# A dense feed-forward in three float32r passes over split weights, inside a two-layer attention and expert kernel

## The chip, the cores and the metric

The kernel runs as one launch on 1 core of a Trainium2 chip. The metric is the time of the launch on the device in microseconds (us), the median of several runs.

## What is computed

The reference takes x (4 x 512 tokens of 512) through four residual steps: a map attention, a token-choice block, a cross attention over 16 heads, and a routed feed-forward with 32 experts. Each takes a layer norm of x. The change lies in the token-choice block, whose dense feed-forward is the last part of this cut:

```python
k = max(1, int(T * CAPACITY))                       # 64 of 512 tokens of each of 4 batches
_, idx = jax.lax.top_k(scores, k)
...
x = sel.reshape(S, D)                               # S = 256 picked rows, D = 512
...                                                 # attention of 16 query and 8 key heads
x1 = x + attn_out
h2 = _rms_norm(x1, ln2_w)
mlp = jax.nn.silu(h2 @ w_gate) * (h2 @ w_up) @ w_down     # 512 x 2048, 512 x 2048, 2048 x 512
processed = x1 + mlp
gated = gate * processed + (1.0 - gate) * x
output = hidden_states.at[b, idx].set(gated.reshape(B, k, D))
```

All inputs and outputs are float32.

## The kernel before

The program is a row of stages (`build`), each with one block of instructions for every engine: `load_constants`, `map_attention`, `token_choice_ffn`, `project_heads`, `context_attention`, `routed_ffn`. X stays in SBUF from stage to stage. At the end of a block all engines meet, and the next block's instructions start together. Inside a block each engine works through its own list in order, and semaphores with increasing counts tie the lists to each other. PSUM is used as 8 banks of 128 x 512 float32.

`token_choice_ffn` (L344) has three blocks. The first picks the 256 rows. The second is the attention, one key head at a time (8 heads); SP loads the slices of `w_o` for it into two buffers (L577) and waits for `out_ready` before it refills one. The third is the dense part (from L736), 256 rows as two groups of 128:

- SP issues all 12 weight loads at once, 1 MB each: for each of 4 parts (512 of the 2048 inner columns) a quarter of `w_gate` and `w_up` (L756) and of `w_down` (L757). All three tensors lie whole in SBUF.
- `rms_turned` (from L504) writes h2 transposed into `b_hT`: ScalarE squares the rows (L513), VectorE and GpSimd make the scale (L521, L529), VectorE scales (L524), TensorE turns 8 blocks (L535), ScalarE multiplies by the norm's weights on the way out of PSUM (L516).
- TensorE, for part n: the gate product into banks 0 and 1, the turn of part n - 1's middle (L819) into banks 4 and 5, the up product into banks 2 and 3 (both L811), and part n - 1's down product (L827) into banks 6 and 7, which add up over all parts. A product is 8 matmuls: 2 groups by 4 slices of 128 of the contraction, each a stationary 128 x 128 block of `b_hT` (or `b_midT`) and 512 moving columns of weights. They are float32; the trace holds two MATMUL records for each.
- ScalarE, in a loop over the parts: silu of the gate product into `b_act_g` (L797), then the turned middle from PSUM into `b_midT` (L801). VectorE, in a loop: `b_mid` = `b_act_g` times the up product (L771).
- Behind the last down product VectorE adds and gates (L776 to L781), TensorE spreads the rows back over the tokens (L848), and VectorE adds them to X (L785).

The routed stage of the same kernel works in float32r already: a number is split into a high part (its float32r rounding, written by a cast) and a low part (the rest, by a subtraction), and a product is three matmuls, high by high, high by low and low by high (L2230, L2235, L2250, L2255).

## Time and profile before

| | us |
|---|---|
| median of 3 runs | 2389.5 (2388.86 to 2392.63) |
| the profiled execution | 2395.94 |
| its span, first to last instruction | 2394.2 |
| TensorE busy | 1989.2 |
| VectorE busy | 1155.8 |
| ScalarE busy | 543.5 |
| mean granted TensorE clock | 0.909 |

The profile is of one execution. PE is TensorE, PEld its weight loads, DVE VectorE, ACT ScalarE, POOL GpSimd, SP SyncE; a q behind a name is the engine's queue of issued instructions. In rows of the trace, `out<-in` names what an instruction writes and reads, and an idle time in brackets is followed by what ended it. Matmuls are pipelined, so the duration of one is longer than the distance to the next; the pace is read from starts. The granted clock is a share of 2.4 GHz. `b_x` in a row stands for `b_x1`.

### The profile page before, as it was taken

How to read it: one execution, taken by the hardware profiler on the slowest of the kernel's cores; microseconds unless marked ns; L12 is line 12 of the kernel's file. 1: busy time of each engine (PE TensorE's matmuls, PEld its weight loads, DVE VectorE, ACT ScalarE, POOL GpSimd, SP SyncE). 2: the span in 40 equal slices, each digit the busy share in tenths (PEclk: the TensorE clock that was granted, in tenths of full speed). 3: DMA queues.
4: the chain of work that ended last, by engine and by line, in shares of the span. 5: the costliest groups of instructions: out<-in, count | busy, mean ns of one | idle time of the engine just before them, and what ended most of it. 6: DMA issues, size and time to landing. Idle time of an engine off the chain costs nothing.

```text
span 2394.2 us, 33404 instructions
## 1 busy us (share of the span) xinstructions
PE 1989.2 (83%) x10468; PEld 1422.6 (59%) x10469; DVE 1155.8 (48%) x2197; ACT 543.5 (23%) x1151; POOL 1141.4 (48%) x566
## 2 busy tenths in 40 slices
PE   5946887969854889999589999999999999999910
PEld 3424443424322333333379999999999999999810
DVE  2564442057673566774773444444444554443300
ACT  3221221101112444443112221122222122222100
POOL 0000000003562455563435557667666878781886
PEclk8977997979985789999789999999999999999965
DMA  3051004121125346711124435554555545543999
GB/s 111 0 147 61 18 27 162 58 80 49 63 83 174 117 163 226 237 51 41 40 88 162 182 118 167 174 159 152 161 163 163 176 160 188 177 163 90 207 158 196
DMA packets 199485, 305.96 MB, mean 128 GB/s; under 512 B 16472, under 2 KB 94808, under 8 KB 199416
## 3 DMA queue, kind: packets, MB, share of 16 engines
q1 hardware_dynamic: 141624, 187.24, 24.8%
q0 software_dynamic: 21504, 50.93, 9.4%
q10 hardware_dynamic: 36288, 66.84, 7.9%
q8 instruction: 45, 0.74, 0.1%
q14 instruction: 24, 0.20, 0.0%
HBM read 186.42 MB, written 118.55 MB: 127 GB/s over the span
## 4 chain that ended last, share of the span: by engine, by line
PE 41%; POOL 5%; DVE 2%; DMA 1%; issue 1%; POOLq 0%; ACT 0%; DVEq 0%
PE psum L2230 16%; PE psum L2250 8%; PE psum L2235 8%; POOL X L1954 5%; PE psum L2255 4%; PE psum L2217 3%; PE psum L2224 2%; DMA X<-d_y,f_slots 1%; DVE f_arena L1175 1%; DVE e_gu_low L2144 0%; DVE f_arena L1165 0%; DVE f_arena L1174 0%; DVE f_arena L1183 0%; DVE e_gu_low L2079 0%; POOLq L1791 0%
## 5 line engine op out<-in xcount | busy, mean ns | idle before, releaser
L2230 PE MATMUL psum<-e_gu_high,e_rowT_high 128*128 (+1 forms) x1272 | 428.0, 339 | 6.3 <-DVE e_gu_low L2144 3.8
L2230 PE MATMUL psum<-e_gu_low,e_rowT_high 128*128 (+1 forms) x1272 | 408.6, 323 | 0.0
L2235 PE MATMUL psum<-e_gu_high,e_rowT_low 128*128 (+1 forms) x1272 | 256.1, 323 | 22.0 <-DVE e_rowT_low L2034 22.0
L1973 ACT ACTIVATE e_silu<-psum 128x352 f32<-128x352 f32 x159 | 73.7, 464 | 879.4 <-PE psum L2235 873.9
L2230 PEld LDWEIGHTS psum<-e_gu_high,e_rowT_high 128*128 128x128 f32 x1272 | 240.7, 189 | 31.1 <-issue 27.0
L2230 PEld LDWEIGHTS psum<-e_gu_low,e_rowT_high 128*128 128x128 f32 x1272 | 241.6, 190 | 3.8
L2235 PEld LDWEIGHTS psum<-e_gu_high,e_rowT_low 128*128 128x128 f32 x1272 | 213.7, 189 | 22.3 <-DVE e_rowT_low L2034 22.3
L2045 DVE TENSOR_TENSOR e_midT_low<-psum,e_midT_high 128x256 fp32r<-128x256 f32 x159 | 67.5, 424 | 325.6 <-ACT e_midT_high L1982 323.4
L2250 PE MATMUL psum<-e_d_high,e_midT_high 128*128 (+3 forms) x477 | 187.7, 394 | 1.0 <-ACT e_midT_high L1982 1.0
L2250 PE MATMUL psum<-e_d_low,e_midT_high 128*128 (+3 forms) x477 | 188.4, 395 | 0.0
L1954 POOL DMA_INDIRECT X<-d_y,f_slots x96 | 148.1, 1542 | 83.3 <-DVE f_arena L2065 52.8
L1904 POOL TENSOR_TENSOR e_gu_high<-f_gu_in,e_ones 128x1408 fp32r<-128x1408 f32 x32 | 81.1, 2534 | 196.2 <-PE psum L2235 178.6
L2065 DVE COPY f_arena<-psum 128x512 f32<-128x512 f32 x127 | 87.8, 692 | 143.4 <-PE psum L2255 140.1
L1405 DVE TENSOR_REDUCE f_hs<-psum 128x2 f32<-128x992 f32 x128 | 151.3, 1182 | 0.0
L1936 POOL DMA_INDIRECT d_sorted<-f_hs,f_slots x96 | 93.7, 976 | 101.8 <-DMA d_sorted<-f_hs,f_slots 63.4
L942 POOL TENSOR_TENSOR x_hrstd<-x_hrstd,minus_half 128x64 f32<-128x64 f32 x8 | 92.3, 11535 | 96.3 <-DVE x_hrstd L960 96.3
L2255 PE MATMUL psum<-e_d_high,e_midT_low 128*128 (+3 forms) x477 | 137.8, 397 | 0.1
L529 POOL TENSOR_TENSOR b_r_ms<-b_r_ms,minus_half 128x2 f32<-128x2 f32 x2 | 1.4, 695 | 241.7 <-DVE b_r_ms L521 241.7
L2034 DVE TENSOR_TENSOR e_rowT_low<-psum,e_rowT_high 128x512 fp32r<-128x512 f32 x159 | 107.7, 677 | 0.0
L2040 DVE SCALAR_TENSOR_TENSOR e_picked<-e_row,f_arena 128x6 f32<-128x6 f32 x127 | 104.2, 821 | 0.0
L1908 POOL TENSOR_TENSOR e_gu_low<-f_gu_in,e_gu_high 128x1408 fp32r<-128x1408 f32 x32 | 103.2, 3225 | 0.0
L1911 POOL TENSOR_TENSOR e_gu_low<-f_gu_in,e_gu_high 128x1408 fp32r<-128x1408 f32 x32 | 102.9, 3216 | 0.0
(348 smaller groups left out, 3787.6 us busy)
## 6 DMA issues: line engine op xcount, KB each, us to landing
d_sorted<-f_hs SPq DMA_DIRECT2D x32, 1048.0 KB, 9.6
e_row<-d_sorted ACTq DMA_DIRECT2D x125, 262.0 KB
d_y<-f_arena ACTq DMA_DIRECT2D x127, 256.0 KB
f_gu_in<-in_L_ffn_w_gate SPq DMA_DIRECT2D x32, 704.0 KB, 5.2
f_gu_in<-in_L_ffn_w_up SPq DMA_DIRECT2D x32, 704.0 KB, 5.1
f_d_in<-in_L_ffn_w_down SPq DMA_DIRECT2D x32, 512.0 KB
d_y<-f_hs SPq DMA_DIRECT2D x8, 1024.0 KB, 5.7
f_d_in<-in_L_ffn_w_down SPq DMA_DIRECT2D x32, 192.0 KB
```

The costliest lines, as they stand in the source:

```text
L942: nc.gpsimd.tensor_tensor(hrstd[:, a, :], hrstd[:, a, :], c.minus_half[:, 0:JT * H], ALU.pow).then_inc(hrstd_ready, 1)
L1405: nc.vector.reduce_max(to[:, :, 0], banks[:, :, 0:MAIN], AX.X, negate=True).then_inc(max_ready, 1)
L1908: nc.gpsimd.tensor_tensor(gu_low[:, par, :, 0:M], gu_in[:, :, 0:M], gu_high[:, par, :, 0:M].bitcast(F32), ALU.subtract).then_inc(gate_spli ...
L1911: nc.gpsimd.tensor_tensor(gu_low[:, par, :, M:2 * M], gu_in[:, :, M:2 * M], gu_high[:, par, :, M:2 * M].bitcast(F32), ALU.subtract).then_i ...
L1936: nc.gpsimd.indirect_dma_start(c.dram["d_sorted"], bass.IndirectOffsetOnAxis(ap=slots[:, k, t:t + 1], axis=0), hs[:, t, :], None).then_inc ...
L1954: nc.gpsimd.indirect_dma_start(c.X[:, t, :], None, c.dram["d_y"], bass.IndirectOffsetOnAxis(ap=slots[:, k, t:t + 1], axis=0), compute_op=A ...
L2034: nc.vector.tensor_tensor(rowT_low[par][:], XT.rearrange("p (k n) -> p k n", k=CC), rowT_high[par][:].bitcast(F32), ALU.subtract).then_inc ...
L2040: nc.vector.scalar_tensor_tensor(picked[par][:], row[par][:, D + TOPK:ROW], expert, row[par][:, D:D + TOPK], ALU.is_equal, ALU.mult, accum ...
L2230: nc.tensor.matmul(bank[:, 0:M].unsqueeze(1), rowT_high[par][:, k, :], w[:, bass.ds(buffer, 1), k, at:at + M], start=(k == 0 and n == 0), ...
L2235: last = nc.tensor.matmul(bank[:, 0:M].unsqueeze(1), rowT_low[par][:, k, :], gu_high[:, bass.ds(buffer, 1), k, at:at + M], start=False, st ...
L2250: nc.tensor.matmul(Y[par].unsqueeze(1), midT_high[0:n, k, :], w[0:n, bass.ds(buffer, 1), k, :], start=(k == 0 and m == 0), stop=False)
L2255: last = nc.tensor.matmul(Y[par].unsqueeze(1), midT_low[0:n, k, :], d_high[0:n, bass.ds(buffer, 1), k, :], start=False, stop=(k == ME - 1))
```

## The change

The 12 slices of the weights become 12 pieces of one size in the order in which TensorE uses them (`PIECES`). A piece is loaded into one of 4 raw buffers; ScalarE casts it to float32r in one of 4 high buffers, VectorE writes raw minus high into one of 4 low buffers, and TensorE makes each product from 24 float32r matmuls: 16 with the high part of `b_hT` (or of the middle) against high and low weights in turn, then 8 with its low part against the high weights. `b_hT` and the middle are split likewise: a cast by ScalarE, a subtraction by VectorE. The lists of ScalarE and VectorE are now written out, without a loop. The first two raw buffers are held from the stage's start, and SP issues their loads in the attention block, behind the third slice of `w_o`. In the dense part SP waits, from piece 4 on, until the low of the piece four before is written. A cast waits for its load, and from piece 4 on for the product of the piece four before.

```diff
@@ -364,6 +368,21 @@
         heads_held = kept.enter_context(ExitStack())
         w_heads = sbuf(nc, heads_held, "b_w_heads", [P, CC, KVH, HEAD_COLS])
         heads_loaded, = sems(nc, c, "b_", "heads_loaded")
+        PARTS = INNER // 512
+        PIECES = [("gate", 0), ("up", 0)]
+        for n in range(1, PARTS):
+            PIECES += [("gate", n), ("up", n), ("down", n - 1)]
+        PIECES += [("down", PARTS - 1)]
+        RAW, RING, EARLY = 4, 4, 2
+        raw = [far_sbuf(nc, kept, f"b_raw{n}", [P, 4, 512]) for n in range(EARLY)]
+        raw_loaded = sems(nc, c, "b_", " ".join(f"raw{n}_loaded" for n in range(RAW)))
+
+        def load_piece(sp, p):
+            kind, n = PIECES[p]
+            cols = slice(n * 512, (n + 1) * 512)
+            src = c.dram["L0_ffn_w_" + kind]
+            src = src[cols, :] if kind == "down" else src[:, cols]
+            sp.dma_start(raw[p % RAW][:], src.rearrange("(k p) n -> p k n", p=P)).then_inc(raw_loaded[p % RAW], 16)
 
         with ExitStack() as stack:
             hs = sbuf(nc, stack, "b_hs", [P, NT, D])
@@ -537,7 +556,7 @@
                 last.then_inc(turned, 1)
                 pe.wait_ge(hT_ready, 1)
 
-            return on_act, on_dve, on_pool, on_pe
+            return on_act, on_dve, on_pool, on_pe, hT_ready
 
         with ExitStack() as stack:
             w_o = sbuf(nc, stack, "b_w_o", [P, 2, QH, D])
...
@@ -576,6 +595,9 @@
                         sp.wait_ge(out_ready, h - 1)
                     sp.dma_start(w_o[:, h % 2], c.dram["L0_ffn_wo"][h * QH * DH:(h + 1) * QH * DH, :].rearrange(
                         "(q d) n -> d q n", d=DH)).then_inc(wo_loaded[h % 2], 16)
+                    if h == 2:
+                        for p in range(EARLY):
+                            load_piece(sp, p)
 
             @block.gpsimd
             def _(pool):
@@ -734,28 +756,27 @@
         heads_held.close()
 
         with ExitStack() as stack:
-            PARTS = INNER // 512
-            w_gate = sbuf(nc, stack, "b_w_gate", [P, CC, INNER])
-            w_up = sbuf(nc, stack, "b_w_up", [P, CC, INNER])
-            w_down = sbuf(nc, stack, "b_w_down", [P, INNER // P, D])
+            raw += [sbuf(nc, stack, f"b_raw{n}", [P, 4, 512]) for n in range(EARLY, RAW)]
+            high, low = [[sbuf(nc, stack, f"b_w_{part}{n}", [P, 4, 512], F32R) for n in range(RING)] for part in ("high", "low")]
             act_g = sbuf(nc, stack, "b_act_g", [P, GROUPS, 512])
             mid = sbuf(nc, stack, "b_mid", [P, GROUPS, 512])
-            midT = sbuf(nc, stack, "b_midT", [P, GROUPS, 512])
-            part_loaded = sems(nc, c, "b_", " ".join(f"part{n}_loaded" for n in range(PARTS)))
+            midT_high, midT_low = [sbuf(nc, stack, f"b_midT_{part}", [P, GROUPS, 512], F32R) for part in ("high", "low")]
+            hT_high, hT_low = [sbuf(nc, stack, f"b_hT_{part}", [P, CC, SLOTS], F32R) for part in ("high", "low")]
             gated, upped, silu_ready, mid_ready, mid_turned, midT_ready, out_ready = sems(
                 nc, c, "b_", "gated upped silu_ready mid_ready mid_turned midT_ready mlp_ready")
             chain_dve, diff_ready, spread, landed = sems(nc, c, "b_", "chain3 diff_ready spread landed")
+            piece_high, piece_low, hT_high_ready, hT_low_ready, midT_low_ready = sems(
+                nc, c, "b_", "piece_high piece_low hT_high_ready hT_low_ready midT_low_ready")
             block = stack.enter_context(nc.Block())
-            rms_act, rms_dve, rms_pool, rms_pe = rms_turned(stack, "b_r2_", x1, mid, 1)
+            rms_act, rms_dve, rms_pool, rms_pe, hT_written = rms_turned(stack, "b_r2_", x1, mid, 1)
 
             @block.sync
             def _(sp):
-                for n in range(PARTS):
-                    cols = slice(n * 512, (n + 1) * 512)
-                    for dst, src in ((w_gate, c.dram["L0_ffn_w_gate"]), (w_up, c.dram["L0_ffn_w_up"])):
-                        sp.dma_start(dst[:, :, cols], src.rearrange("(k p) n -> p k n", p=P)[:, :, cols]).then_inc(part_loaded[n], 16)
-                    sp.dma_start(w_down[:, n * 4:(n + 1) * 4, :], c.dram["L0_ffn_w_down"].rearrange("(k p) n -> p k n", p=P)[
-                        :, n * 4:(n + 1) * 4, :]).then_inc(part_loaded[n], 16)
+                for p in range(EARLY, len(PIECES)):
+                    if p >= RAW:
+
+                        sp.wait_ge(piece_low, p - RAW + 1)
+                    load_piece(sp, p)
 
             @block.gpsimd
             def _(pool):
@@ -763,15 +784,45 @@
 
             @block.vector
             def _(dve):
-                rms_dve(dve)
-                with dve.Fori(0, PARTS) as n:
+                def low_of(*pieces):
+                    for p in pieces:
+                        dve.wait_ge(piece_high, p + 1)
+                        nc.vector.tensor_tensor(low[p % RING][:], raw[p % RAW][:], high[p % RING][:].bitcast(F32), ALU.subtract).then_inc(piece_low, 1)
+
+                def multiply(n):
                     dve.wait_ge(silu_ready, n + 1)
                     dve.wait_ge(upped, n + 1)
                     for g in range(GROUPS):
                         last = nc.vector.tensor_tensor(mid[:, g, :], act_g[:, g, :], c.bank[2 + g][:], ALU.mult)
                     last.then_inc(mid_ready, 1)
+
+                def low_midT(n):
+                    dve.wait_ge(midT_ready, n + 1)
+                    for g in range(GROUPS):
+                        last = nc.vector.tensor_tensor(midT_low[:, g, :], c.bank[4 + g][:], midT_high[:, g, :].bitcast(F32), ALU.subtract)
+                    last.then_inc(midT_low_ready, 1)
+
+                low_of(0, 1)
+                rms_dve(dve)
+                dve.wait_ge(hT_high_ready, 1)
+                nc.vector.tensor_tensor(hT_low[:], hT[:], hT_high[:].bitcast(F32), ALU.subtract).then_inc(hT_low_ready, 1)
+                low_of(2, 3)
+                multiply(0)
+                low_of(4)
+                low_midT(0)
+                low_of(5)
+                multiply(1)
+                low_of(6, 7)
+                low_midT(1)
+                low_of(8)
+                multiply(2)
+                low_of(9, 10)
+                low_midT(2)
+                low_of(11)
+                multiply(3)
+                low_midT(3)
                 chain = Chain(dve, chain_dve)
-                dve.wait_ge(out_ready, 1)
+                dve.wait_ge(out_ready, PARTS)
                 for g in range(GROUPS):
                     last = nc.vector.tensor_tensor(x1[:, g, :], x1[:, g, :], c.bank[6 + g][:], ALU.add)
                 chain.link(last)
@@ -789,57 +840,102 @@
 
             @block.scalar
             def _(act):
-                rms_act(act)
-                with act.Fori(0, PARTS) as n:
+                def high_of(*pieces):
+                    for p in pieces:
+                        act.wait_ge(raw_loaded[p % RAW], 16 * (p // RAW + 1))
+                        if p >= RING:
+
+                            kind, n = PIECES[p - RING]
+                            act.wait_ge({"gate": gated, "up": upped, "down": out_ready}[kind], n + 1)
+                        nc.scalar.copy(high[p % RING][:], raw[p % RAW][:]).then_inc(piece_high, 1)
+
+                def silus(n):
                     act.wait_ge(gated, n + 1)
-
                     for g in range(GROUPS):
                         last = nc.scalar.activation(act_g[:, g, :], c.bank[g][:], ACT.Silu)
                     last.then_inc(silu_ready, 1)
+
+                def copy_midT(n):
                     act.wait_ge(mid_turned, n + 1)
                     for g in range(GROUPS):
-                        last = nc.scalar.copy(midT[:, g, :], c.bank[4 + g][:])
+                        last = nc.scalar.copy(midT_high[:, g, :], c.bank[4 + g][:])
                     last.then_inc(midT_ready, 1)
+
+                high_of(0, 1)
+                rms_act(act)
+                act.wait_ge(hT_written, 1)
+                nc.scalar.copy(hT_high[:], hT[:]).then_inc(hT_high_ready, 1)
+                high_of(2, 3)
+                silus(0)
+                high_of(4)
+                copy_midT(0)
+                silus(1)
+                high_of(5, 6, 7)
+                copy_midT(1)
+                silus(2)
+                high_of(8, 9, 10)
+                copy_midT(2)
+                silus(3)
+                high_of(11)
+                copy_midT(3)
 
             @block.tensor
             def _(pe):
                 rms_pe(pe)
-
-                def product(at, w, n):
+                pe.wait_ge(hT_high_ready, 1)
+
+                def product(at, p):
+                    pe.wait_ge(piece_low, p + 1)
                     for g in range(GROUPS):
+                        rows = slice(g * P, (g + 1) * P)
                         for k in range(CC):
-                            last = nc.tensor.matmul(c.bank[at + g][:], hT[:, k, g * P:(g + 1) * P],
-                                                    w[:, k, n * 512:(n + 1) * 512], start=(k == 0), stop=(k == CC - 1))
+                            for m, w in enumerate((high, low)):
+                                nc.tensor.matmul(c.bank[at + g][:], hT_high[:, k, rows], w[p % RING][:, k, :], start=(k == 0 and m == 0), stop=False)
+                    pe.wait_ge(hT_low_ready, 1)
+                    for g in range(GROUPS):
+                        rows = slice(g * P, (g + 1) * P)
+                        for k in range(CC):
+                            last = nc.tensor.matmul(c.bank[at + g][:], hT_low[:, k, rows], high[p % RING][:, k, :], start=False, stop=(k == CC - 1))
                     return last
 
                 def turn_mid(n):
                     pe.wait_ge(mid_ready, n + 1)
+                    if n >= 1:
+                        pe.wait_ge(midT_low_ready, n)
                     for g in range(GROUPS):
                         for k in range(4):
                             last = nc.tensor.transpose(c.bank[4 + g][:, k * P:(k + 1) * P], mid[:, g, k * P:(k + 1) * P], c.ident[:])
                     last.then_inc(mid_turned, 1)
 
-                def down(n):
+                def down(n, p):
 
                     pe.wait_ge(midT_ready, n + 1)
+                    pe.wait_ge(piece_low, p + 1)
                     for g in range(GROUPS):
                         for k in range(4):
-                            last = nc.tensor.matmul(c.bank[6 + g][:], midT[:, g, k * P:(k + 1) * P], w_down[:, n * 4 + k, :],
-                                                    start=(n == 0 and k == 0), stop=(n == PARTS - 1 and k == 3))
+                            for m, w in enumerate((high, low)):
+                                nc.tensor.matmul(c.bank[6 + g][:], midT_high[:, g, k * P:(k + 1) * P], w[p % RING][:, k, :],
+                                                 start=(n == 0 and k == 0 and m == 0), stop=False)
+                    pe.wait_ge(midT_low_ready, n + 1)
+                    for g in range(GROUPS):
+                        for k in range(4):
+                            last = nc.tensor.matmul(c.bank[6 + g][:], midT_low[:, g, k * P:(k + 1) * P], high[p % RING][:, k, :],
+                                                    start=False, stop=(n == PARTS - 1 and k == 3))
                     return last
 
...
+                for p, (kind, n) in enumerate(PIECES):
+                    if kind == "gate":
+                        if n >= 1:
+                            pe.wait_ge(silu_ready, n)
+                        product(0, p).then_inc(gated, 1)
+                    elif kind == "up":
+                        if n >= 1:
+                            turn_mid(n - 1)
+                        product(2, p).then_inc(upped, 1)
+                    else:
+                        if n == PARTS - 1:
+                            turn_mid(n)
+                        down(n, p).then_inc(out_ready, 1)
```

Three places in the engines' lists, in the program's order (names as in the code, `x` the count, L the line of the kernel that is listed).

ScalarE in the dense part, before (L793 is the loop over the parts, so L797 and L801 run four times):

```order
L790 UNCONDITIONAL_BRANCH
L513 ACTIVATE b_mid,b_r_ms<-b_x 128x512 x2
L516 ACTIVATE b_hT<-psum,b_ln_w 128x256 x4
L793 UNCONDITIONAL_BRANCH
L793 ISA
L797 ACT_TABLE_LOAD
L797 ACTIVATE b_act_g<-psum 128x512 x2
L801 COPY b_midT<-psum 128x512 x2
```

and after (the start and the first two parts):

```order
L841 UNCONDITIONAL_BRANCH
L850 CAST b_w_high<-b_raw 128x2048 x2
L532 ACTIVATE b_mid,b_r_ms<-b_x 128x512 x2
L535 ACTIVATE b_hT<-psum,b_ln_w 128x256 x4
L867 CAST b_hT_high<-b_hT 128x1024
L850 CAST b_w_high<-b_raw 128x2048 x2
L855 ACT_TABLE_LOAD
L855 ACTIVATE b_act_g<-psum 128x512 x2
L850 CAST b_w_high<-b_raw 128x2048
L861 CAST b_midT_high<-psum 128x512 x2
L855 ACTIVATE b_act_g<-psum 128x512 x2
L850 CAST b_w_high<-b_raw 128x2048 x3
```

Two casts of weights stand ahead of the squares, one of `b_hT` behind its writing, and the others between silu and the copy of the middle.

VectorE at the same place, before:

```order
L764 UNCONDITIONAL_BRANCH
L521 TENSOR_SCALAR b_r_ms<-b_r_ms 128x2
L524 TENSOR_SCALAR b_mid<-b_x,b_r_ms 128x512 x2
L767 UNCONDITIONAL_BRANCH
L767 ISA
L771 TENSOR_TENSOR b_mid<-b_act_g,psum 128x512 x2
```

and after:

```order
L785 UNCONDITIONAL_BRANCH
L790 TENSOR_TENSOR b_w_low<-b_raw,b_w_high 128x2048 x2
L540 TENSOR_SCALAR b_r_ms<-b_r_ms 128x2
L543 TENSOR_SCALAR b_mid<-b_x,b_r_ms 128x512 x2
L808 TENSOR_TENSOR b_hT_low<-b_hT,b_hT_high 128x1024
L790 TENSOR_TENSOR b_w_low<-b_raw,b_w_high 128x2048 x2
L796 TENSOR_TENSOR b_mid<-b_act_g,psum 128x512 x2
L790 TENSOR_TENSOR b_w_low<-b_raw,b_w_high 128x2048
L802 TENSOR_TENSOR b_midT_low<-psum,b_midT_high 128x512 x2
```

Two subtractions stand ahead of the scale of the norm, and every later one between the two steps of the middle.

SP from the attention block to the dense part, after (before, the 8 loads of `w_o` stand together and the 12 weight loads behind them):

```order
L596 DMA b_w_o<-in_L_ffn_wo 128x2x512 x3
L385 DMA b_raw<-in_L_ffn_w_gate 128x4x512
L385 DMA b_raw<-in_L_ffn_w_up 128x4x512
L596 DMA b_w_o<-in_L_ffn_wo 128x2x512 x5
L561 UNCONDITIONAL_BRANCH
L773 UNCONDITIONAL_BRANCH
L385 DMA b_raw<-in_L_ffn_w_gate 128x4x512
L385 DMA b_raw<-in_L_ffn_w_up 128x4x512
L385 DMA b_raw<-in_L_ffn_w_down 128x4x512
```

The first two pieces come between `w_o`'s third and fourth slice, and the rest begin with piece 2.

## Rows read from the trace of the kernel before

**Rows 1.** The page, part 1: busy us (share of the span) x instructions.
```profile
PE 1989.2 (83%) x10468; PEld 1422.6 (59%) x10469; DVE 1155.8 (48%) x2197; ACT 543.5 (23%) x1151; POOL 1141.4 (48%) x566
```

**Rows 2.** Windows of the core: us, busy of each engine, granted clock, DMA share, GB/s.
```profile
393.50:404.30 10.80, 1.97 (x8) 1.57 (x8) 1.05 (x3) 4.18 (x9) 0.69 (x1) 0.53 0.90 323
404.30:498.00 93.70, 88.92 (x225) 40.88 (x226) 8.53 (x13) 12.49 (x19) 0.00 (x0) 0.97 0.26 97
404.30:426.00 21.70, 21.64 (x47) 9.56 (x48) 1.28 (x2) 1.08 (x2) 0.00 (x0) 0.92 1.05 387
1600.00:2000.00 400.00, 399.97 (x2365) 368.94 (x2364) 195.46 (x416) 81.04 (x236) 293.58 (x132) 1.00 0.52 166
```

**Rows 3.** Waits between 380 and 520 us: who <- whom: us, times, longest.
```profile
DVE b_mid L771 <- PE psum L811: 76.9, 4, 23.2
```

**Rows 4.** Timeline, 393 to 414 us: start, us, engine, line, operation, [idle before <-releaser].
```profile
393.75 0.63 ACT L513 ACTIVATE b_mid<-b_x 128x512 f32<-128x512 f32 x1 [7.73 <-PEq L542]
...
395.11 0.17 DVE L521 TENSOR_SCALAR b_r_ms<-b_r_ms 128x2 f32<-128x2 f32 x1 [1.67 <-ACT b_mid L513]
...
397.03 1.97 PE L535 MATMUL psum<-ident,b_mid 128*128 128x128 f32 x8 [4.91 <-DVE b_mid L524]
399.04 1.57 ACT L516 ACTIVATE b_hT<-psum,b_ln_w 128x256 f32<-128x256 f32 x4 [3.96 <-PE psum L535]
...
404.36 8.86 PE L811 MATMUL psum<-b_w_gate,b_hT 128*128 128x512 f32 x16 [5.36 <-DMA b_w_down<-in_L_ffn_w_down]
...
413.06 1.45 PE L811 MATMUL psum<-b_w_up,b_hT 128*128 128x512 f32 x3
```

**Rows 5.** Timeline of TensorE, 419 to 500 us.
```profile
419.92 7.03 PE L811 MATMUL psum<-b_w_gate,b_hT 128*128 128x512 f32 x16
426.79 1.04 PE L819 MATMUL psum<-ident,b_mid 128*128 128x128 f32 x8
427.66 7.03 PE L811 MATMUL psum<-b_w_up,b_hT 128*128 128x512 f32 x16
...
486.55 7.13 PE L827 MATMUL psum<-b_w_down,b_midT 128*128 128x512 f32 x16 [1.16 <-ACT b_midT L801]
```

**Rows 6.** Timeline of TensorE in the routed stage, the float32r down product.
```profile
1220.55 0.39 PE L2250 MATMUL psum<-e_d_high,e_midT_high 128*128 128x512 f32 x1
...
1221.94 0.87 PE L2255 MATMUL psum<-e_d_high,e_midT_low 128*128 128x512 f32 x3
```

**Rows 7.** Groups of ScalarE and VectorE by form: x count | busy us, mean ns | idle before.
```profile
L1977 ACT CAST e_rowT_high<-psum 128x512 fp32r<-128x512 f32 x159 | 96.2, 605 | 0.7 <-PE psum L2217 0.7
...
L2006 ACT CAST e_gu_high<-f_gu_in 128x1408 fp32r<-128x1408 f32 x2 | 2.7, 1388 | 0.0
...
L2006 ACT CAST e_d_high<-f_d_in 128x1024 fp32r<-128x1024 f32 x1 | 1.1, 1061 | 0.0
...
L2034 DVE TENSOR_TENSOR e_rowT_low<-psum,e_rowT_high 128x512 fp32r<-128x512 f32 x159 | 107.7, 677 | 0.0
...
L969 DVE TENSOR_TENSOR x_q<-x_q,x_affine 128x2048 f32<-128x2048 f32 x8 | 18.3, 2292 | 0.3
...
L2079 DVE TENSOR_TENSOR e_gu_low<-f_gu_in,e_gu_high 128x1408 fp32r<-128x1408 f32 x2 | 3.2, 1618 | 0.0
L2144 DVE TENSOR_TENSOR e_gu_low<-f_gu_in,e_gu_high 128x1408 fp32r<-128x1408 f32 x1 | 2.9, 2889 | 8.8 <-ACT e_gu_high L2009 8.8
...
L2079 DVE TENSOR_TENSOR e_d_low<-f_d_in,e_d_high 128x1024 fp32r<-128x1024 f32 x1 | 1.2, 1219 | 0.0
```

**Rows 8.** The tile b_w_gate: from issue to landing.
```profile
DMA to landing us min/median/max: 5.1/13.0/15.4
```

**Rows 9.** Line 687 (the w_o products): what its idle time waited for: us, times.
```profile
  ACT b_oT L662: 2.9, 2
```

**Rows 10.** Timeline of TensorE in the routed stage at the low clock.
```profile
1210.98 0.49 PE L2230 MATMUL psum<-e_gu_high,e_rowT_high 128*128 128x352 f32 x1
1211.27 0.49 PE L2230 MATMUL psum<-e_gu_low,e_rowT_high 128*128 128x352 f32 x1
```

More of the change, by code:

```diff
@@ L562, in token_choice_ffn @@
             block = stack.enter_context(nc.Block())
[L563 removed]
+            rms_act, rms_dve, rms_pool, rms_pe, _ = rms_turned(stack, "b_r1_", picked, qkv[:, 0], 0)
             SCALE = DH ** -0.5
```

15 lines of the change are left out of this document (2 added, 13 removed).

## The prediction

> **What bounds the kernel now.** The page gives the whole: TensorE is busy 83% of the span [rows 1]. That share is a mean over stages, and the page's chain of waits is followed back through only about half of the span, so it says nothing of this stage. I read the stage itself in this order: the windows, to see who works in it; the timeline of its start; the timeline of TensorE inside it; what VectorE and ScalarE wait for; and then, from the routed stage of the same kernel, what the three-pass form costs there.
>
> The dense part runs from 393.5 to 498 us [rows 2]. From 404.3 to 498.0 TensorE is busy 88.9 of 93.7 us, VectorE 8.5 and ScalarE 12.5. VectorE waits 76.9 us there for the products [rows 3]. So TensorE's stream is the bound, and the two engines that the change burdens are nearly idle. Ahead of it stands the start [rows 4]: ScalarE squares at 393.75, VectorE goes on at 395.11, TensorE turns the rows at 397.03, ScalarE has b_hT at 400.61. Then TensorE waits 3.75 us more for the three loads of part 0 and begins at 404.36. Every later stage begins behind a barrier on all engines, so what this stage saves goes to the end one for one.
>
> **The products.** Now a piece (8 fp32 matmuls of 512 columns, 16 records) takes 426.79 - 419.92 = 6.87 us [rows 5], 0.429 us per record. After, a piece is 24 float32r matmuls of 512 columns. The routed stage runs just this form, a high and a low moving operand in turn against one stationary: seven of 512 columns start one behind the other from 1220.55 to 1221.94, six steps of 0.232 us [rows 6]. 24 x 0.232 = 5.57 us, a gain of 1.30 us per piece and 15.6 us for 12. The transposes stay (426.79 to 427.66, 0.87 us a time), as does the wait of 1.2 us for the last ScalarE copy.
>
> Here the nearest rows allow another value. Half of an fp32 record is 0.2146 us, so 24 could take 5.15 us; I take 0.232 because it is the same form, types and shape. The Trainium skill, TensorE: Matmul & The Clock Gate, section "Back-to-back issue gap", gives columns / 2.4 + 2.5 ns for an isolated gap, 216 ns at 512 columns. By that page a piece would be an estimated 5.2 us and the stage's gain near 20 us; this trace disagrees for float32r, where it shows 232 ns. Above, the bound is the half clock, below under the rivals.
>
> **The start.** Now ScalarE casts pieces 0 and 1 before it squares, and VectorE forms both lows before it touches the mean square. One cast of 2048 columns: 1.061 us at 1024 and 1.388 at 1408 [rows 7] is 0.85 ns a column more, so 1.93 us. One subtraction on VectorE: 1.219 and 1.618 us at the same widths, so 2.29 us at 2048, as the 2.292 of a plain one on 2048. The bound above is the lone 2.889 us at 1408 columns (4.1 us at 2048), taken beside a busy GpSimd, which this stage does not have; below, nothing shows it faster than 2.2.
>
> The chain: casts end at 395.7 and 397.6, squares at 398.9, lows at 398.0 and 400.3. VectorE is the later one, so its step of 395.11 starts at 400.3, 5.2 us late. From there to b_hT is 5.5 us as before: 405.8. The cast to hT_high (1024 columns) adds 1.06: TensorE starts at 407.0 instead of 404.36, **2.6 us later**. The old wait for part 0's loads hid part of this; the lead of pieces 0 and 1, loaded among the heads, is what keeps it so small. Without that lead the first cast would start only when a load issued at 393.7 had landed, 5.1 us later at the earliest [rows 8], and all behind it with it. hT_low (1.22 us) lies beside the 16 matmuls that come first. TensorE still starts at the low clock (first matmuls 1.2 GHz, granted 0.53 between 393.5 and 404.3 [rows 2]) and loses 1.8 us to it: its first piece took 8.7 us, not 6.87. The idle stretch before it shrinks from 5.4 to 2.9 us; I leave that loss as it is.
>
> **The stream behind it.** Operations of 512 columns from PSUM take 0.605 us on ScalarE and 0.677 on VectorE [rows 7]. Per part, ScalarE has three casts and four of those (silu, middle copy): 8.2 us. VectorE has three subtractions and four of those (products, middle lows): 9.6. TensorE has 3 x 5.57 + 0.87 = 17.6. A cast waits until the product four pieces back has left its buffer; TensorE then has three pieces (16.7 us) before it needs the result, and cast plus subtraction take 4.2. Walked through in the order of the instructions, piece 2 has its low at 411 and TensorE asks at 420; piece 5 at 433 for 437.5; piece 8 at 450.5 for 455; and the last middle is written at 469.4 (behind the last piece's low, on VectorE) for a turn at 472.7. So the tightest slack is 3.3 us and no piece is waited for. Only one table load of 1.28 us remains of four on ScalarE; none was on the path.
>
> Loads: at 387 GB/s between 404.3 and 426.0 [rows 2] 1 MB takes 2.7 us against 5.6 us of TensorE's. SP's wait for a low holds back only later loads; piece 4 is issued at 398 and cast at 417. The two early loads stand on SP ahead of five loads of w_o, each issued a head (some 20 us) before use, and the w_o products wait for ScalarE alone now [rows 9]: nothing.
>
> **Sum.** -15.6 + 2.6 = -13.0 us. The profiled execution took 2395.9 (span 2394.2), 6.4 above the median of the three runs, 2389.5; its own forecast is 2382.9 (span 2381.2), and taken off the median **2376.5 us**. A measurement here can tell about 0.2%, or 4.8 us, from no change.
>
> **Rivals.**
> - *float32r at the pace of an fp32 pass.* The 0.2146 above, 5.15 us a piece: -20.6 + 2.6 = -18 us, 2371.5. For it: the fp32 records run at that pace [rows 5]; against: the rows of this very form [rows 6]. 9%. (The Trainium skill's page on TensorE, named above, has this spacing.)
> - *Subtractions at 4.1 us* (the 2.889 row). Two of them at the start make TensorE 3.6 us later again; in the stream VectorE has 15 us a part and stays under 17.6. -9.4 us: 2380.1. Against: GpSimd has 0.7 us of work here. 8%.
> - *TensorE waits for pieces.* In-order engines turn a late silu into a late cast into a late product. 0.8 us at each of 12 pieces leaves -3.4: 2386. Against: slack of 3.3 us and more everywhere. 7%.
> - *Slower: the half clock inside the stream.* If TensorE falls to 1.2 GHz, a 352-column float32r matmul takes 0.293 us between starts instead of 0.16 [rows 10], so one of 512 an estimated 0.42 and a piece 10.1 us, 4.5 more. Three pieces at that clock eat the gain; with six it is +14: 2404. It would need gaps in the stream: the row that shows it follows 22 us in which TensorE waited. Against: the granted clock was 1.00 over 1600 to 2000 us of the same form [rows 2], and no gap is foreseen. 4%.
> - *The matmuls do not run in one pass* (the types do not take effect): 0.429 each, 10.3 us a piece, +44: 2433. Nothing here speaks for it. 1%.
>
> **Numbers.** Forecast 71%. The range 2370 to 2385 takes in the first two rivals and about 2 us of scatter (the runs lie 3.8 apart), and leaves out the last three. Faster by over 0.2%: 71 + 9 + 8 = 88%; within it 7%; slower 5%.
>
> **What would show it.** TensorE's first product near 407.0; pieces 5.6 us apart with starts every 0.23 us; no wait of TensorE for b_w_low or b_mid; casts near 1.93 and subtractions near 2.29 us; b_hT_high written near 406.9; the last product ending near 480.6 instead of 493.7; and every later stage 13 us earlier, unchanged in length. A piece spacing over 6.5 us, or a start behind 411, would make the forecast wrong.

## The result, and the profile after

| | before | changed |
|---|---|---|
| median of 5 runs, us | 2391.3 (2388.9 to 2393.8) | 2373.7 (2372.4 to 2379.1) |
| span of the profiled execution | 2394.2 | 2373.3 |

The ratio is 0.993, 95% interval 0.9915 to 0.9945: 13 to 20 us faster. Forecast were 13.0 us less and 2376.5 us, between 2370 and 2385.

The page after, its span and the busy times:

```profile
span 2373.3 us, 33616 instructions
...
PE 1965.8 (83%) x10564; PEld 1439.7 (61%) x10565; DVE 1189.8 (50%) x2218; ACT 562.1 (24%) x1161; POOL 1141.6 (48%) x566
```

TensorE's busy share is 83% in both [rows 1]: its busy time (1989.2 and 1965.8 us) fell with the span. The windows of the dense part, to the first product and from there to the last (columns as in [rows 2]):

```profile
393.50:406.60 13.10, 1.97 (x8) 1.59 (x9) 5.51 (x6) 7.63 (x12) 0.70 (x1) 0.52 0.87 319
406.60:479.40 72.80, 71.55 (x320) 58.90 (x320) 33.61 (x28) 27.53 (x27) 0.00 (x0) 0.97 0.26 87
```

The same stretch before, from the first product to the add behind the last:

```profile
404.30:493.70 89.40, 88.16 (x224) 40.38 (x224) 5.14 (x8) 12.49 (x19) 0.00 (x0) 0.98 0.28 102
```

TensorE is busy 71.6 of 72.8 us where it was 88.2 of 89.4, and VectorE works 33.6 us beside it instead of 5.1. What waits now (who <- whom: us, times, longest; the answer to [rows 3]):

```profile
ACT b_midT_high L861 <- PE psum L907: 36.3, 4, 9.8
...
DVE b_w_low L790 <- ACT b_w_high L850: 7.3, 5, 2.2
DVE b_mid L796 <- PE psum L898: 7.1, 1, 7.1
...
PE psum L893 <- issue: 2.8, 1, 2.8
...
PE psum L917 <- ACT b_midT_high L861: 1.2, 1, 1.2
```

VectorE still waits for TensorE's products (once, 7.1 us; before, 76.9 in four waits), and TensorE waits for no low weights and no middle: its two waits are the start and the last copy. The start, in the timeline (the answer to [rows 4]):

```profile
393.62 3.70 ACT L850 CAST b_w_high<-b_raw 128x2048 fp32r<-128x2048 f32 x2 [7.64 <-PEq L561]
...
395.54 4.49 DVE L790 TENSOR_TENSOR b_w_low<-b_raw,b_w_high 128x2048 fp32r<-128x2048 f32 x2 [2.23 <-ACT b_w_high L850]
397.22 0.63 ACT L532 ACTIVATE b_mid<-b_x 128x512 f32<-128x512 f32 x1
...
399.95 0.16 DVE L540 TENSOR_SCALAR b_r_ms<-b_r_ms 128x2 f32<-128x2 f32 x1
...
401.87 1.97 PE L554 MATMUL psum<-ident,b_mid 128*128 128x128 f32 x8 [9.87 <-DVE b_mid L543]
403.87 1.57 ACT L535 ACTIVATE b_hT<-psum,b_ln_w 128x256 f32<-128x256 f32 x4 [5.32 <-PE psum L554]
...
405.47 1.04 ACT L867 CAST b_hT_high<-b_hT 128x1024 fp32r<-128x1024 f32 x1
...
406.62 0.77 PE L893 MATMUL psum<-b_w_high,b_hT_high 128*128 128x512 f32 x1 [2.78 <-issue]
```

The two casts and the two subtractions stand ahead of the norm; VectorE's step of 395.11 comes at 399.95, and the first product at 406.62. The stream, TensorE's timeline (the answer to [rows 5]; the first three rows are the third pass of the first three products):

```profile
412.45 2.00 PE L898 MATMUL psum<-b_w_high,b_hT_low 128*128 128x512 f32 x8
...
417.91 1.98 PE L898 MATMUL psum<-b_w_high,b_hT_low 128*128 128x512 f32 x8
...
423.35 1.99 PE L898 MATMUL psum<-b_w_high,b_hT_low 128*128 128x512 f32 x8
...
471.39 1.04 PE L907 MATMUL psum<-ident,b_mid 128*128 128x128 f32 x8
473.59 0.50 PE L917 MATMUL psum<-b_w_high,b_midT_high 128*128 128x512 f32 x1 [1.16 <-ACT b_midT_high L861]
...
482.89 1.22 PE L944 MATMUL psum<-b_x,b_slot_hot_T 128*128 128x512 f32 x1 [3.56 <-DVE b_x L832]
```

From 417.91 to 423.35 is one piece: 5.44 us, or 0.2267 us for each of 24 matmuls, where a piece took 6.87. The costs of the split, as groups:

```profile
L790 DVE TENSOR_TENSOR b_w_low<-b_raw,b_w_high 128x2048 fp32r<-128x2048 f32 x12 | 27.1, 2288 | 7.3 <-ACT b_w_high L850 7.3
...
L850 ACT CAST b_w_high<-b_raw 128x2048 fp32r<-128x2048 f32 x12 | 22.3, 1918 | 7.6 <-PEq L561 7.6
```

To compare profiles whose earlier stages differ by a microsecond or two, I count from the first ScalarE instruction of the dense block (393.75 before, 393.62 changed; from SP's first issue where ScalarE starts with a wait) to the first product, to the add behind the last product (L776, now L827), and to the start of the next stage (its first VectorE instruction). All in us:

| kernel | first product | final add | next stage |
|---|---|---|---|
| before (three profiles) | 10.6, 10.6, 10.7 | 100.0, 100.0, 100.0 | 127.6, 127.6, 127.7 |
| changed (three profiles) | 13.0, 13.0, 13.0 | 85.8, 85.8, 85.7 | 112.7, 112.7, 112.7 |
| two passes only (e1) | 13.0 | 64.5 | 91.3 |
| norm first (e2) | 8.0 | 81.5 | 108.2 |
| no lead (e3) | 18.6 | 91.9 | 118.6 |
| no lead, norm first (e4) | 12.3 | 85.4 | 112.2 |
| lows made twice (e5) | 13.0 | 85.7 | 112.6 |
| GpSimd kept busy (e6) | 16.3 | 89.2 | 116.1 |
| float32 with lead (e7) | 6.9 | 96.4 | 123.1 |
| norm first, high rows direct (e8) | 6.9 | 79.3 | 106.0 |

So the stage gained 127.6 - 112.7 = **15.0 us** (14.96 before rounding), repeatable to 0.1. The rest of the 17.6 lies outside it; what can be said of it stands under the repeats.

The table also tells the two parts of the change apart. In float32 the early loads alone save 4.5 us (e7). The three passes without them save 127.6 - 118.6 = 9.0 us (e3). Together they save 15.0: the lead is worth 5.9 us once the casts stand ahead of the norm, because the first cast then waits for a load.

### The profile page after: what moved, and what is told of

Read it like the earlier page. It is cut to its first block, busy times and chain, and to the rows that moved or that the text cites. A ratio compares the mean times of both kernels' runs of the same rounds, so it can differ in the third digit from the quotient of the medians.

```text
span 2373.3 us, 33616 instructions
## 1 busy us (share of the span) xinstructions
PE 1965.8 (83%) x10564; PEld 1439.7 (61%) x10565; DVE 1189.8 (50%) x2218; ACT 562.1 (24%) x1161; POOL 1141.6 (48%) x566
## 4 chain that ended last, share of the span: by engine, by line
PE 42%; POOL 5%; DVE 2%; DMA 2%; issue 1%; POOLq 0%; ACT 0%; DVEq 0%
PE psum L2326 16%; PE psum L2346 9%; PE psum L2331 8%; POOL X L2050 5%; PE psum L2351 4%; PE psum L2313 3%; PE psum L2320 2%; DMA X<-d_y,f_slots 2%; DVE f_arena L1271 1%; DVE e_gu_low L2240 0%; DVE f_arena L1261 0%; DVE f_arena L1270 0%; DVE f_arena L1279 0%; DVE e_gu_low L2175 0%; POOLq L1887 0%
## 5 line engine op out<-in xcount | busy, mean ns | idle before, releaser
L2136 DVE SCALAR_TENSOR_TENSOR e_picked<-e_row,f_arena 128x6 f32<-128x6 f32 x127 | 105.6, 831 | 0.0
L2004 POOL TENSOR_TENSOR e_gu_low<-f_gu_in,e_gu_high 128x1408 fp32r<-128x1408 f32 x32 | 103.2, 3225 | 0.0
L2351 PEld LDWEIGHTS psum<-e_d_high,e_midT_low 128*128 128x128 f32 (+1 forms) x477 | 89.8, 189 | 21.8 <-DVE e_midT_low L2143 0.9
```

Of the source, the lines that this page charges most:

```text
L2004: nc.gpsimd.tensor_tensor(gu_low[:, par, :, 0:M], gu_in[:, :, 0:M], gu_high[:, par, :, 0:M].bitcast(F32), ALU.subtract).then_inc(gate_spli ...
L2136: nc.vector.scalar_tensor_tensor(picked[par][:], row[par][:, D + TOPK:ROW], expert, row[par][:, D:D + TOPK], ALU.is_equal, ALU.mult, accum ...
L2351: last = nc.tensor.matmul(Y[par].unsqueeze(1), midT_low[0:n, k, :], d_high[0:n, bass.ds(buffer, 1), k, :], start=False, stop=(k == ME - 1))
```

## The experiments

**e1: is TensorE's stream the bound?** The third pass is left out (the low part of the rows and of the middle against the high weights), so the result lacks those terms; every split is still made and waited for. The down product is cut in the same way.

```diff
                             for m, w in enumerate((high, low)):
-                                nc.tensor.matmul(c.bank[at + g][:], hT_high[:, k, rows], w[p % RING][:, k, :], start=(k == 0 and m == 0), stop=False)
+                                last = nc.tensor.matmul(c.bank[at + g][:], hT_high[:, k, rows], w[p % RING][:, k, :], start=(k == 0 and m == 0), stop=(k == CC - 1 and m == 1))
                     pe.wait_ge(hT_low_ready, 1)
-                    for g in range(GROUPS):
-                        rows = slice(g * P, (g + 1) * P)
-                        for k in range(CC):
-                            last = nc.tensor.matmul(c.bank[at + g][:], hT_low[:, k, rows], high[p % RING][:, k, :], start=False, stop=(k == CC - 1))
```

> Leaves out the third pass of every dense product (low part of the rows against the high weights); all splits are still made and waited for. Stream theory (TensorE's matmuls are the bound, 0.227 us each): first product at 406.6 us as in the changed kernel, then 8 x 12 matmuls less, -21.8 us; walked through, the last turn waits 0.8 us more, so the final add starts near 458.5 us instead of 479.4. Split theory (casts, subtractions and their waits set the pace): the final add moves by less than 10 us.

The final add came at 458.52, 21.2 us less counted from the block's start, for 96 matmuls less (21.8 at 0.227): this is what the stream theory said. Only at the last turn did VectorE hold TensorE for a moment (timeline; the middle is written at 450.91 to 452.19, the turn starts at 452.29 after 0.24 us of waiting):

```profile
450.91 1.28 DVE L796 TENSOR_TENSOR b_mid<-b_act_g,psum 128x512 f32<-128x512 f32 x2
...
452.29 1.06 PE L903 MATMUL psum<-ident,b_mid 128*128 128x128 f32 x8 [0.24 <-issue]
...
454.52 0.50 PE L913 MATMUL psum<-b_w_high,b_midT_high 128*128 128x512 f32 x1 [1.16 <-ACT b_midT_high L861]
...
458.52 1.28 DVE L827 TENSOR_TENSOR b_x<-b_x,psum 128x512 f32<-128x512 f32 x2 [2.73 <-PE psum L913]
```

**e5: how much slack has VectorE?**

```diff
+                        if p >= 2:
+                            nc.vector.tensor_tensor(low[p % RING][:], raw[p % RAW][:], high[p % RING][:].bitcast(F32), ALU.subtract).then_inc(twice, 1)
+                            dve.wait_ge(twice, p - 1)
                         nc.vector.tensor_tensor(low[p % RING][:], raw[p % RAW][:], high[p % RING][:].bitcast(F32), ALU.subtract).then_inc(piece_low, 1)
```

> Every weight subtraction from piece 2 on is made twice on VectorE, 2.25 us more each. Slack theory (TensorE asks 3.3 us or more behind each low and middle): VectorE rises to 16.5 us a part against TensorE's 17.2, and the final add stays within 1 us of 479.4, seen from the same block start. Rival (in-order coupling between VectorE and TensorE is already tight): the final add moves by 5 to 22 us.

```profile
L793 DVE TENSOR_TENSOR b_w_low<-b_raw,b_w_high 128x2048 fp32r<-128x2048 f32 x12 | 27.4, 2292 | 2.6 <-ACT b_w_high L853 2.2
...
L791 DVE TENSOR_TENSOR b_w_low<-b_raw,b_w_high 128x2048 fp32r<-128x2048 f32 x10 | 22.9, 2288 | 4.4 <-ACT b_w_high L853 4.4
...
480.95 1.28 DVE L830 TENSOR_TENSOR b_x<-b_x,psum 128x512 f32<-128x512 f32 x2 [4.51 <-PE psum L925]
```

Ten more subtractions (L791), 22.9 us more work on VectorE, and final add (480.95, the block's start being 395.21) and next stage did not move (85.7, 112.6). The split rivals fall with e1 and e5: beside the stream, the split costs nothing. ScalarE's share was not made longer in any run; that it keeps up in e1, where a product has 16 matmuls instead of 24, is what speaks for its slack.

**e2: what does the order at the start cost?** ScalarE squares and VectorE scales before either touches the weights; the two casts run between the squares and the wait for the turned rows.

```diff
-                low_of(0, 1)
                 rms_dve(dve)
+                low_of(0, 1)
...
-                high_of(0, 1)
-                rms_act(act)
+                rms_act(act, lambda: high_of(0, 1))
```

> The changed kernel with the squares ahead of the first two casts on ScalarE and the norm's scale ahead of the first two subtractions on VectorE. If the delay of the start is these four pieces of work standing ahead of the norm: VectorE's scale back at 395.0 us instead of 399.95, first product near 401.6 to 402 instead of 406.6, the final add near 474.4, and the whole about 5 us faster than the changed kernel. Rival (the start is bound by the later lows or by hT_low, so the order only moves the wait): first product stays behind 405 us and the total is unchanged.

```profile
393.93 0.63 ACT L532 ACTIVATE b_mid<-b_x 128x512 f32<-128x512 f32 x1 [7.76 <-PEq L562]
...
395.17 3.68 ACT L851 CAST b_w_high<-b_raw 128x2048 fp32r<-128x2048 f32 x2
395.30 0.17 DVE L541 TENSOR_SCALAR b_r_ms<-b_r_ms 128x2 f32<-128x2 f32 x1 [1.67 <-ACT b_mid L532]
...
397.09 4.49 DVE L791 TENSOR_TENSOR b_w_low<-b_raw,b_w_high 128x2048 fp32r<-128x2048 f32 x2
...
401.97 0.77 PE L893 MATMUL psum<-b_w_high,b_hT_high 128*128 128x512 f32 x1 [2.78 <-ACT b_hT_high L867]
```

VectorE's step is back at 1.4 us behind the block's start, the first product 5.0 us earlier (8.0 instead of 13.0), the final add 4.2. Part of the gain goes to the clock: here TensorE's matmuls ran at 0.43 us a start for 6.1 us from 401.97, in the changed kernel for 4.4 us from 406.62. The total, 2372.9 (2369.1 to 2377.5), does not show these 4 us against 2373.7: in the profiled executions the routed stage began only 3.1 us earlier (1153.5 against 1156.6), since the context attention took 436.8 us here and 434.0 there (the stage between took 1.8 us less).

**e3 and e4: what are the two early loads worth?** `RAW, RING, EARLY = 4, 4, 0` instead of `4, 4, 2`, in the changed kernel and in norm-first.

> No piece is loaded among the heads; all 12 loads are issued in the dense block. Theory (the lead is worth the landing of the first load, since the norm stands behind the first two casts on ScalarE): first cast at 393.6 + 5 to 6 us = near 399, first product near 412 to 413, final add near 485 us, 6 us later than in the changed kernel. Rival (the lead is hidden as the loads were before, worth under 2 us): first product by 408.

```profile
392.39 0.37 SPq L385 DMA_DIRECT2D b_raw<-in_L_ffn_w_gate  x1
...
397.43 1.90 ACT L850 CAST b_w_high<-b_raw 128x2048 fp32r<-128x2048 f32 x1 [12.68 <-DMA b_raw<-in_L_ffn_w_gate]
...
400.14 1.90 ACT L850 CAST b_w_high<-b_raw 128x2048 fp32r<-128x2048 f32 x1 [0.82 <-DMA b_raw<-in_L_ffn_w_up]
...
410.94 0.77 PE L893 MATMUL psum<-b_w_high,b_hT_high 128*128 128x512 f32 x1 [2.78 <-issue]
```

The first cast starts 5.0 us behind the issue, the second waits for its load too, and the first product comes 5.5 us later than with the lead (18.6 against 13.0), the next stage 5.9.

> Norm-first order, and no piece loaded among the heads. ScalarE squares at once, then waits for the first load (5 us behind its issue) and the second, and has the rows to write only behind those two casts: b_hT_high near 11.9 us behind the block's start, against 8.0 with the lead and 13.2 to 13.5 measured for no lead in the old order counted to the high part. So the lead is worth 3.5 to 4 us in this order too, because the casts still stand ahead of the rows on ScalarE. Rival (with the norm ahead, the loads are hidden and the lead is worth nothing): first product within 0.5 us of the 8.04 us of the norm-first kernel, counted from the block's start.

```profile
405.87 0.77 PE L893 MATMUL psum<-b_w_high,b_hT_high 128*128 128x512 f32 x1 [7.04 <-ACT b_hT_high L867]
```

The 13.2 to 13.5 us that this expectation gives for e3 are counted from e3's first cast (397.43); from the start of its block b_hT_high was written 18.4 us later. Measured here: first product 12.3 against 8.0, next stage 112.2 against 108.2. The lead is worth 4 us in this order as well.

**e7: the lead alone, in the kernel before.** Part 0 of w_gate and w_up gets two buffers of its own, loaded behind the third slice of w_o, and the gate product waits for those alone; the products stay float32.

```diff
+                    if h == 2:
+                        for dst, src in zip(w_lead, (c.dram["L0_ffn_w_gate"], c.dram["L0_ffn_w_up"])):
+                            sp.dma_start(dst[:], src[:, 0:512].rearrange("(k p) n -> p k n", p=P)).then_inc(lead_loaded, 16)
...
-                    pe.wait_ge(part_loaded[n], 3 * 16)
+                    pe.wait_ge(lead_loaded, 2 * 16) if n == 0 else pe.wait_ge(part_loaded[n], 3 * 16)
+                    if n == 1:
+                        pe.wait_ge(part_loaded[0], 16)
```

> The kernel before, with float32 products, but part 0 of w_gate and w_up loaded among the heads into buffers of their own; the gate product no longer waits for part 0 of w_down. It shows what the lead alone gives without the split: TensorE's first product moves from 404.36 to about 400.7 us, right behind b_hT, and the final add from 493.7 to about 490.0; so 3.7 us of the old time is this wait, and the three passes have to give the other 11. Rival (the lead costs the attention block, whose w_o loads stand behind 2 MB): the dense block starts later than 394.5 us.

First product 6.9 us behind the block's start instead of 10.6, final add 3.6 earlier, next stage 4.5 earlier. So 4.5 us of the stage's gain can be had without any float32r. The block did start late, at 395.88, but before itself started it at 396.40 in a repeat, so that is no price of the loads. Its one time, 2395.5, lies above before's although its dense part is 4.5 us shorter: its context attention took 441.0 us, the longest of the lengths below, and one time of this kernel decides nothing at this size.

**e6: why 0.227 us here and 0.232 in the routed stage?** GpSimd multiplies 1024 columns 20 times, behind its own step of the norm (a power).

```diff
                 rms_pool(pool)
+                for n in range(20):
+                    nc.gpsimd.tensor_tensor(idle_out[:], idle_in[:], idle_in[:], ALU.mult).then_inc(idle_set, 1)
+                    pool.wait_ge(idle_set, n + 2)
```

> The changed kernel with 20 multiplications of 1024 float32 columns added on GpSimd behind its power of the norm, into a buffer that nobody reads. Question: why the float32r matmuls start every 0.227 us here and every 0.232 us in the routed stage. Theory A (GpSimd's SBUF traffic of the routed stage costs TensorE the 5 ns): spacing 0.231 to 0.233 while GpSimd works, final add 1 to 1.5 us later. Theory B (nothing to do with GpSimd; it lies in the mix of matmul shapes or the DMA traffic there): spacing stays 0.2265 to 0.2275. Side question: do the subtractions of 2.29 us stretch beside GpSimd as the lone 2.889 us one seemed to? If they do, 4 us and more each; if not 2.3.

```profile
L790 POOL TENSOR_TENSOR b_idle_out<-b_idle_in 128x1024 f32<-128x1024 f32 x20 | 52.4, 2618 | 1.5
L798 DVE TENSOR_TENSOR b_w_low<-b_raw,b_w_high 128x2048 fp32r<-128x2048 f32 x12 | 35.5, 2985 | 6.7 <-ACT b_w_high L858 6.7
...
L543 DVE TENSOR_SCALAR b_mid<-b_x,b_r_ms 128x512 f32<-128x512 f32 x2 | 4.1, 2109 | 0.9 <-POOL b_r_ms L548 0.9
```

Theory A fell: pieces stayed at 5.44 us, and from first product to final add it took 72.9 us (72.8 changed). VectorE paid: subtractions 2.99 us in the mean (3.98 at most) instead of 2.29, and the norm's two scalings 2.1 us each instead of 0.49. That sits on the start's chain, so the first product came 3.3 us later. The prediction's bound of 4.1 us for a subtraction beside GpSimd is nearly reached here (3.98), but not in the changed kernel. The Trainium skill, SBUF — State Buffer, section "SBUF: two separate sides", says that VectorE and GpSimd share a pair of SBUF ports under an exclusive lock, which VectorE needs for operations in a two-port mode or, against a GpSimd operation that reads SBUF, with two inputs in SBUF, while TensorE and ScalarE never wait for it; by that page this is the pattern to expect, and the run agrees (TensorE 72.9 us, ScalarE's casts 1.9 us).

What makes 0.232 is not settled. In the dense part itself, the first matmuls after the rise of the clock or after a turn started 0.2325 us apart (e1: eight from 411.95 to 413.81), and the later ones 0.2267. The routed stage has at most about nine such matmuls in a row. That fits, but no run tried it, and "the first eight" is no fixed number: behind the rise of the clock in e2 and e8 only two starts were 0.232 apart (408.34 and 408.57; 403.30 and 403.53). Two windows of the changed kernel speak against the DMA traffic of theory B (columns as in [rows 2]):

```profile
413.50:415.50 2.00, 2.00 (x11) 1.65 (x10) 0.00 (x0) 1.02 (x3) 0.00 (x0) 1.00 1.07 407
...
473.90:475.20 1.30, 1.30 (x7) 1.05 (x6) 0.96 (x2) 0.00 (x0) 0.00 (x0) 1.00 0.00 0
```

In the first the DMA engines move 407 GB/s and matmuls start every 0.227 us; in the second they move nothing and the starts are 0.232 apart.

**e8: the best of these.** Norm first, and ScalarE writes the high part of the rows from PSUM (turned into banks 4 and 5), VectorE the low part.

```diff
-                nc.scalar.copy(hT_high[:], hT[:]).then_inc(hT_high_ready, 1)
...
+                for k in range(CC):
+                    last = nc.vector.scalar_tensor_tensor(hT_low[:, k, :], c.bank[4 + k // 2][:, (k % 2) * SLOTS:(k % 2 + 1) * SLOTS], ln_w[:, 1, k:k + 1],
+                                                          hT_high[:, k, :].bitcast(F32), ALU.mult, ALU.subtract)
+                last.then_inc(hT_low_ready, 1)
```

> The norm-first order, and ScalarE writes the high part of the rows straight from PSUM while VectorE forms the low part from PSUM in four steps of 256 columns (the turned rows lie in banks 4 and 5). Theory: the 1.04 us cast leaves the chain, first product near 400.9 us against 401.97 in the norm-first kernel, final add 1 us earlier, near 474.4. Rival: VectorE's four steps (0.4 to 0.5 us each, behind the two lows) end behind the first 16 matmuls and TensorE waits for the low part: no gain or a loss.

```profile
397.77 1.57 ACT L536 ACTIVATE b_hT_high<-psum,b_ln_w 128x256 fp32r<-128x256 f32 x4 [0.36 <-PE psum L555]
...
399.39 0.80 PE L893 MATMUL psum<-b_w_high,b_hT_high 128*128 128x512 f32 x1 [1.66 <-ACT b_hT_high L536]
...
400.05 1.65 DVE L810 SCALAR_TENSOR_TENSOR b_hT_low<-psum,b_ln_w,b_hT_high 128x256 fp32r<-128x256 f32 x4
```

The cast has left the chain (first product 6.9, 1.1 us less), and the low part is done at 401.70, far ahead of 404.90, where the seventeenth matmul is the first to read it. The final add came 2.2 us earlier than in e2 and not 1: the low clock lasted 3.6 us behind the first product instead of 6.1. The next stage starts 6.6 us earlier than in the changed kernel. In the same set of runs it took 2369.2 us (2367.1 to 2374.1) against 2376.4 (2374.3 to 2382.5) for the changed kernel: 7 us. Against before it is 0.990 (0.9885 to 0.9916), the fastest of the kernels that leave nothing out.

**Repeats: where do the other microseconds come from?** The same programs again.

> The changed kernel itself, once more. Question: which part of the 17.6 us belongs to the change and which to scatter behind it. In the first two profiles the dense part and the spreading behind it ended 15.1 us earlier, but the routed stage began 20.7 us earlier, and the stretch from the first y_q_high cast to the first routed product took 440.9 us before and 434.0 after. Scatter theory: that stretch has no fixed length for a given program, so this second profile of the same program shows another one, 2 us or more away from 434.0, while everything up to the next stage's start (506.3 us) repeats within 1.5 us once the start of the dense block is taken off. Rival (the stretch depends on where the change put it): 434 within 1 us again.

> The kernel before, once more. From the start of its dense block to the start of the next stage it took 127.6 us (the changed kernel: 112.7 in both of its profiles), and should again, within 0.3. The open question is the context attention: its first heads came 22 to 26 us apart in a few fixed patterns, with the granted clock between 0.50 and 0.90, and the stretch from the first y_q_high cast to the first routed product took 440.9 us (before), 434.0 (changed, twice), and 430.8 to 441.0 in the experiments. Phase theory (a pattern is drawn by how the clock's ups and downs fall, not by the program): another of the lengths 431, 434, 437 or 441 comes up for the same program in one of these two repeats of before. Rival (each program has its own length): 441 each time.

> As the last one: 127.6 us from dense block to the next stage within 0.3; phase theory: a length of the context attention other than 441 in this or the last; rival: 441.

> The changed kernel a third time: 112.7 us from the start of the dense block to the next stage. Phase theory: a length of the context attention other than 434 may come up; rival: 434 again.

The dense part repeats to 0.1 us. The context attention does not: from the first y_q_high cast to the first routed product, before took 440.9, 433.9 and 436.7 us. In the windows of before, the second part of that stretch, first profile and then first repeat:

```profile
916.40:1177.30 260.90, 229.87 (x1607) 97.59 (x1605) 171.56 (x327) 105.57 (x134) 127.13 (x53) 0.96 0.36 115
```

```profile
919.60:1173.40 253.80, 222.80 (x1588) 94.82 (x1589) 170.17 (x325) 105.21 (x134) 125.59 (x52) 0.98 0.36 117
```

The same work (VectorE 171.6 and 170.2 us, ScalarE 105.6 and 105.2) takes 260.9 us at a granted clock of 0.96 and 253.8 at 0.98. Over the whole stretch VectorE is busy 272.2 us in all three, and TensorE 371.1, 363.7 and 366.5 us for the same 2600 matmuls; the granted clock was at its low level for 106.4, 92.5 and 98.8 us of it. At half the pace those 13.9 and 7.6 us are worth 7.0 and 3.8, and the lengths differ by 7.1 and 4.2. The changed kernel took 434.0, 434.0 and 434.0. I had expected its second profile to differ; it did not, and that spoke for a length of its own until the repeats of before showed that the program does not fix the length. Why the changed kernel drew 434 three times stays open.

So the first two profiles can be added up. The routed stage began 20.7 us earlier (1177.3 and 1156.6): 15.0 from the dense part, 0.1 from the block's earlier start, 6.9 from the context attention's draw, less 1.4 by which the stage between them took longer (20.65 unrounded). Of the 17.6 us between the medians, 15.0 are shown to be the change. The interval of 13 to 20 holds 15.0, so the other 2.6 need no cause. But a second set of runs gave 18.0 us (2394.3 and 2376.4, interval 14 to 20), again 3 us more, and from the next stage's start to the first routed product the three profiles of before took 655.9, 649.4 and 652.4 us and those of the changed kernel 650.3 each time. Whether the changed kernel's shift in time also draws a shorter length behind it, no run here settles.

## Why the prediction was right, step by step

- **The bound.** Right. e1 and e5 show it from both sides.
- **The products.** Foreseen 15.6 us, measured 12 x (6.87 - 5.44) = 17.2. The term was mis-sized by its spacing, 0.232 taken from the routed stage against 0.2267. From the first product to the final add the gain is 89.4 - 72.8 = 16.6, so 0.6 us came back. 0.4 of it is the first piece, which took 7.7 us (from 406.62 to 414.28), 2.2 over the later ones and not 1.8 as before: the low clock lasted 4.4 us behind the first product, where it had lasted 3.5.
- **The start.** Foreseen 2.6 us later, measured 13.0 - 10.6 = 2.4. Casts 1.92 us and subtractions 2.29 (foreseen 1.93 and 2.29).
- **The stream behind it.** Right: the last middle was written at 468.06 and turned at 471.39, 3.3 us of slack as walked through. No piece was waited for. Of TensorE's two waits, the one for the last copy is the 1.2 us that the prediction kept.
- **Not in the sum:** 0.7 us in the spreading (L848, now L944), whose code is unchanged. Behind the start of its matmuls the granted clock was 0.50 for 6 us before (497.2 to 503.2) and for 3 us now (482.9 to 485.9), and the repeats of both kernels show the same.
- **The sum.** -13.0 foreseen. The products gave 1.6 us more and 0.6 of it came back, the start cost 0.2 less than foreseen, and the spreading gave 0.7: within rounding the -15.0 of the dense part and its spreading. The total of -17.6 goes beyond it by 2.6 us that no term foresaw. That the time of 2373.7 lies only 2.8 us from the 2376.5 is in part luck: the gain was 4.6 us larger than the forecast, but the median of before in five runs was 1.8 us above that of the three runs from which the forecast took it. "Goes to the end one for one" holds as far as the next stage's start; behind it the lengths scatter by 7 us.
- **The rivals.** The 0.2146 spacing would have given 5.15 us a piece; 5.44 stands between it and the 5.57 of the forecast. Subtractions of 4.1 us: none in the changed kernel (2.29); up to 3.98 in e6 alone. TensorE waiting for pieces: no. The half clock inside the stream: granted 0.97 there, the low stretch only at the start; a float32r matmul of 512 columns started every 0.427 us in it, as estimated (0.42). The types did take effect.

## What to carry to other kernels

Three float32r passes over split operands beat float32 by 1.4 us per 8 matmuls of 512 columns as long as the splitting fits beside TensorE's stream: here VectorE could do ten of its twelve weight subtractions twice for nothing. The price is at the stage's start, where the first splits stand ahead of whatever chain releases the first product; put that chain first (4.5 us here) and load the first pieces a stage early (4 to 6 us, of which 4.5 could be had in float32 too). Judge a change of this size by the stage counted from its own start, since the five totals of the changed kernel alone lie 7 us apart.

## What was not expected of the hardware

- A stage of unchanged code took 434, 437 or 441 us in three profiles of one program, with TensorE's granted clock at the lower of its two levels (1.2 and 2.4 GHz) for 93, 99 and 106 us of it.
- float32r matmuls of 512 columns started every 0.2267 us in long rows. The first ones behind the rise of the clock started every 0.232 us: nine in the changed kernel, e1 and e6, two in e2 and e8; behind the last turn of the changed kernel it was five. Neither a busy GpSimd nor the DMA traffic makes the difference; what does stays open.
- A busy GpSimd stretched a VectorE scaling of 512 columns from 0.49 to 2.1 us and left TensorE's pace untouched.
- After the first product the low clock (1.2 GHz) lasted 3.5 us before, 4.4 in the changed kernel, 6.1 in e2 and 3.6 in e8; TensorE had waited 5.4, 2.8, 2.8 and 1.7 us before it.
